# Where the weighted LoRA rows are split into high and low parts: before the transposes or behind them

## What is computed

```
xn  = layernorm(x)
K,V = elu(xn wk.T + bk) + 1, xn wv.T + bv;  KV = sum over the tokens of K V      (16 heads of 32)
out = Q KV / (Q sum K + 1e-8), then wo.T + bo;  Q = elu(xn wq.T + bq) + 1
s   = sigmoid(xn W_router) (8 experts); the best 2 of s + expert_bias get weights s / (sum of the two + 1e-8)
gate/up = xn W + (xn sA) sB / 8 + sum over experts of weight * (xn A_e) B_e / 8   (rank 8, width 1376)
ffn = (silu(gate) * up) W_down + the same LoRA terms of the down side
y   = x + attention + ffn
```

## Time and profile before

| What | Value |
|---|---|
| median of 3 runs | 721.21 us (720.41 to 721.88) |
| the profiled execution | 720.7 us, its span 718.9 us |
| TensorE busy | 701.2 us (98%) |
| VectorE busy | 376.2 us (52%) |
| ScalarE busy | 260.7 us (36%) |
| GpSimd busy | 122.3 us (17%) |
| granted clock of TensorE | 1.0 in the whole span |

### The profile page before, as it was taken

How to read it: one execution, slowest core, us unless ns; L and a number is a source line. 1 busy time by engine, 2 the same in 40 slices (tenths; PEclk the granted TensorE clock), 3 DMA queues, 4 the chain that set the end, 5 groups by cost and what they waited for, 6 DMA issues and landing times.

```text
span 718.9 us, 10792 instructions
## 1 busy us (share of the span) xinstructions
PE 701.2 (98%) x3690; PEld 563.2 (78%) x3690; DVE 376.2 (52%) x715; ACT 260.7 (36%) x402; POOL 122.3 (17%) x293
## 2 busy tenths in 40 slices
PE   7999999989999999999999999999999999999997
PEld 5788888876776677888888888888888888888886
DVE  5666556677575675444427444336534435544434
ACT  4344334564331432333333333324333224323322
POOL 3554555420642651000000000000000000000000
PEclk9999999999999999999999999999999999999999
DMA  7756656326746635000010500001600001300001
GB/s 241 270 194 195 202 192 210 125 111 251 274 142 236 221 131 217 18 0 0 0 49 37 208 0 0 0 4 54 233 0 0 0 0 58 117 0 0 0 0 60
DMA packets 22755, 72.79 MB, mean 101 GB/s; under 512 B 2688, under 2 KB 2944, under 8 KB 20688
## 3 DMA queue, kind: packets, MB, share of 16 engines
q1 hardware_dynamic: 22560, 72.24, 28.4%
q0 software_dynamic: 176, 0.30, 0.2%
HBM read 51.56 MB, written 20.97 MB: 101 GB/s over the span
## 4 chain that ended last, share of the span: by engine, by line
PE 90%; DVE 4%; issue 2%; POOL 2%; ACT 1%; DMA 1%; SPq 0%; DVEq 0%; POOLq 0%; ACTq 0%
PE bank L1115 19%; PE bank L1116 19%; PE bank L1117 19%; PE bank L1328 17%; PE bank L1303 6%; PE bank L1315 4%; PE bank L1228 2%; DMA w_raw<-in_wkT 1%; PE bank L1180 1%; PE bank L1132 1%; PE bank L1152 1%; PE bank L1144 1%; PE bank L1236 1%; PE bank L1344 0%; PE bank L1346 0%
## 5 line engine op out<-in xcount | busy, mean ns | idle before, releaser
L1115 PE MATMUL bank<-x,up_h 128*128 (+1 forms) x352 | 137.5, 391 | 2.1 <-DVE qf L980 1.2
L1116 PE MATMUL bank<-x,up_h 128*128 (+1 forms) x352 | 137.3, 390 | 0.0
L1117 PE MATMUL bank<-x,up_l 128*128 (+1 forms) x352 | 137.0, 389 | 0.0
L1048 DVE TENSOR_TENSOR hf<-bank,silu 128x512 f32<-128x512 f32 x44 | 30.4, 692 | 162.3 <-issue 142.6
L1115 PEld LDWEIGHTS bank<-x,up_h 128*128 128x128 f32 x352 | 66.1, 188 | 18.8 <-issue 2.1
L597 ACT ACTIVATE hid_h<-hf 128x512 fp32r<-128x512 f32 x44 | 27.8, 632 | 142.9 <-DVE hf L1048 142.9
L1117 PEld LDWEIGHTS bank<-x,up_l 128*128 128x128 f32 x352 | 66.1, 188 | 14.1
L1116 PEld LDWEIGHTS bank<-x,up_h 128*128 128x128 f32 x352 | 66.1, 188 | 13.8
L793 DVE TENSOR_TENSOR up_l<-up_raw,up_h 128x1024 fp32r<-128x1024 f32 x45 | 55.6, 1235 | 31.4 <-ACT up_h L597 31.4
L1328 PE MATMUL bank<-dn_h,hid_h 128*128 128x512 f32 x176 | 69.5, 395 | 0.0
L1328 PE MATMUL bank<-dn_l,hid_h 128*128 128x512 f32 x176 | 69.1, 392 | 0.0
(11 more groups left out here) (167 smaller groups left out, 1228.3 us busy)
## 6 DMA issues: line engine op xcount, KB each, us to landing
x<-scr_x SPq DMA_DIRECT2D x8, 2048.0 KB, 7.5
up_raw<-in_ffn_up SPq DMA_DIRECT2D x11, 768.0 KB, 5.5
scr_x<-xt SPq DMA_DIRECT2D x16, 512.0 KB, 4.4
xin<-in_x SPq DMA_DIRECT2D x16, 256.0 KB, 5.8
scr_z<-zt SPq DMA_DIRECT2D x16, 256.0 KB, 2.2
x3r<-in_x SPq DMA_DIRECT2D x16, 256.0 KB, 3.5
scr_att<-x3r SPq DMA_DIRECT2D x16, 256.0 KB, 2.1
z<-scr_z SPq DMA_DIRECT2D x4, 1024.0 KB, 5.0
```

What stands on the lines that cost most here:

```text
L1048: nc.vector.tensor_tensor(hf[:], ps_u[:], silu[:], ALU.mult).then_inc(h_done, 1)
L1115: nc.tensor.matmul(dst, lh, rh, start=start, stop=False, **kw)
L1116: nc.tensor.matmul(dst, lh, rl, start=False, stop=False, **kw)
L1117: return nc.tensor.matmul(dst, ll, rh, start=False, stop=stop, **kw)
```

## The change

The weighted rows are written unrounded into `zst`, now one block of 128 columns a side, the shared ones three times in the same operation. Two transposes a tile, one a side, take the place of four. The split is made behind them: ScalarE rounds the transposed rows from PSUM to `zt` in two operations (all 128 rows as the second block, the upper 64 as the first block's high half), and VectorE's `lora_lo` writes the low parts to partitions 64 to 127: a subtraction for the first block, and for the second one operation that multiplies the rounded rows by a mask (-1 for the 8 low rows, 0 elsewhere) and adds the transposed ones. The store now waits for VectorE. `lora_hi` is gone, `lora_lo` works on tile t-2 in the stage of tile t, and behind the stage it has new places. The low shared rows move by 8, and the prepared weights with them.

```diff
@@ -58,7 +58,7 @@
-SL = ER + R
+SL = ER + 2 * R
...
-        zf = at("zf", [P, 2, ER])
-        zs = at("zs", [P, 2, R])
-        zst = at("zst", [P, 2, 2, P], F32R)
+        zst = at("zst", [P, 2, P])
+        zmask = at("zmask_sb", [P, 1])
         zt = at("zt", [P, 2 * 2, P], F32R)
+        zt4 = zt[:].rearrange("p (a b) n -> p a b n", b=2)
...
-            nc.gpsimd.memset(zst[:].bitcast(F32), 0.0)
+            nc.gpsimd.memset(zst[:], 0.0)
...
             pool.dma_start(bq_c[:], dram["bq"]).then_inc(consts_in, 16)
+            pool.dma_start(zmask[:], dram["zmask"]).then_inc(consts_in, 16)
...
-            def lora_hi(t):
-
-                act.wait_ge(zf_done, t + 1)
-                round_to(zst[:, :, :, 0:ER], zf[:].unsqueeze(2).to_broadcast([P, 2, 2, ER]))
-                round_to(shared_cols(zst), zs[:].unsqueeze(2).to_broadcast([P, 2, 2, R])).then_inc(zhi_done, 1)
-
             def lora_out(t):
                 act.wait_ge(zt_ready, t + 1)
                 act.wait_ge(scr_zd, 16 * (t + 1))
-                round_to(zt[:].rearrange("p k n -> p (k n)"), ps_zt[:]).then_inc(zt_done, 1)
+                pst = ps_zt[:, 0:2 * P].rearrange("p (a n) -> p a n", a=2)
+                round_to(zt4[:, :, 1], pst)
+                round_to(zt4[0:ER, :, 0], pst[0:ER]).then_inc(zhi_done, 1)
...
-                if behind(t, 1):
-                    lora_hi(t - 1)
...
-            def stack_lo(st, zf_, zs_):
-
-                sub(st[:, :, 0, ER:2 * ER], zf_[:], st[:, :, 0, 0:ER])
-                return sub(st[:, :, 1, SL:SL + R], zs_[:], st[:, :, 1, SH:SH + R])
-
...
                 dve.wait_ge(route_done, t + 1)
-                nc.vector.tensor_scalar(zs[:], zraw[:, 2 * ER:2 * ER + 2 * R].rearrange("p (a r) -> p a r", a=2),
-                                        RSCALE, None, ALU.mult)
+                wait(dve, zt_ready, t)
+                shared = zraw[:, 2 * ER:2 * ER + 2 * R].rearrange("p (a o r) -> p a o r", a=2, o=1)
+                nc.vector.tensor_scalar(zst[:, :, SH:].rearrange("p a (b c) -> p a b c", c=2 * R)[:, :, 0:3, 0:R],
+                                        shared.to_broadcast([P, 2, 3, R]), RSCALE, None, ALU.mult)
...
-                        zf[:, a:a + 1].rearrange("p a (e r) -> p a e r", e=E),
+                        zst[:, a:a + 1, 0:ER].rearrange("p a (e r) -> p a e r", e=E),
                         zraw[:, a * ER:(a + 1) * ER].rearrange("p (a e r) -> p a e r", a=1, e=E), weight, ALU.mult)
-                last.then_inc(zf_done, 1)
+                last.then_inc(zst_done, 1)
 
             def lora_lo(t):
-                dve.wait_ge(zf_done, t + 1)
+
                 dve.wait_ge(zhi_done, t + 1)
-                stack_lo(zst, zf, zs).then_inc(zst_done, 1)
+                pst = ps_zt[:, 0:2 * P].rearrange("p (a n) -> p a n", a=2)
+                sub(zt4[ER:, :, 0], pst[0:ER], zt4[0:ER, :, 0])
+                nc.vector.scalar_tensor_tensor(zt4[ER:, :, 1], zt4[ER:, :, 1].bitcast(F32), zmask[ER:], pst[ER:], ALU.mult, ALU.add
+                                               ).then_inc(zt_done, 1)
...
-                if not first:
-                    lora_lo(t - 1)
+                if behind(t, 2):
+                    lora_lo(t - 2)
                 dve.wait_ge(z_ready, t + 1)
+                wait(dve, zst_done, t)
                 nc.vector.tensor_copy(zraw[:], ps_z[:, 0:NZ]).then_inc(zraw_done, 1)
...
-            dve.wait_ge(consts_in, 64)
+            dve.wait_ge(consts_in, 80)
...
             queries(0, (0,))
+            lora_lo(TILES - 2)
             m_lo(0, (2, 3))
...
             lora_weighted(TILES - 1)
-            lora_lo(TILES - 1)
...
             dve.wait_ge(rr_clear, 1)
+            lora_lo(TILES - 1)
             m_lo(1, (0, 1))
...
                 pe.wait_ge(zst_done, t + 1)
-                for k in range(4):
-                    last = nc.tensor.transpose(ps_zt[:, k * P:(k + 1) * P], zst[:, k // 2, k % 2, :].bitcast(F32), ident[:])
+                wait(pe, zt_done, t)
+                for k in range(2):
+                    last = nc.tensor.transpose(ps_zt[:, k * P:(k + 1) * P], zst[:, k, :], ident[:])
                 last.then_inc(zt_ready, 1)
...
+    zmask = np.zeros((P, 1), f32)
+    zmask[SL:SL + R] = -1.0
```

More of the change, by code:

```diff
@@ L60 @@
     "ffn_up": (P, FC, UPC), "ffn_dn": (P, FC, DNC), "b_dn": (P, 2, D),
-    "ident": (P, P), "headmask": (P, HC), "headcol": (P, KD, HEADS), "headrow": (P, KD, P), "earlier": (1, E, E),
+    "ident": (P, P), "headmask": (P, HC), "headcol": (P, KD, HEADS), "headrow": (P, KD, P), "earlier": (1, E, E), "zmask": (P, 1),
 }
@@ L249, in program @@
         rexp_done = sem("rexp_done")
-        zf_done = sem("zf_done")
         zhi_done = sem("zhi_done")
@@ L597, in round_to @@
                 return nc.scalar.activation(dst, src, ACT.Copy)
-            def shared_cols(st):
-                return st[:, :, 1, SH:].rearrange("p a (b c) -> p a b c", c=32)[:, :, :, 0:R]
             def tokens_hi(t, s, uses):
@@ L715, in _ @@
             queries(0, (1,))
-            lora_hi(TILES - 1)
             queries(0, (2, 3))
@@ L1405, in experts_out, with blocks @@
         return b.reshape(ER, b.shape[2])
-    def blocks(b, shared):
+    def blocks(b, shared, low=SL):
         full = np.zeros((P, 2, b.shape[1]), f32)
         full[0:ER, 0] = full[ER:2 * ER, 0] = full[0:ER, 1] = b
-        full[SH:SH + R, 1] = full[SL:SL + R, 1] = full[SH2:SH2 + R, 1] = shared
+        full[SH:SH + R, 1] = full[low:low + R, 1] = full[SH2:SH2 + R, 1] = shared
         return full
@@ L1438 @@
         "ffn_up": ffn_up, "ffn_dn": chunked(padded(ffn_dn, wide, DNC)),
-        "b_dn": blocks(experts_out(given["B_down"]), given["sB_down"]),
+        "b_dn": blocks(experts_out(given["B_down"]), given["sB_down"], ER + R),
         "ident": np.eye(P, dtype=f32), "headmask": np.repeat(np.eye(HC, dtype=f32), DK, axis=0),
         "headcol": headcol, "headrow": headrow,
-        "earlier": np.tril(np.ones((E, E), f32), -1).reshape(1, E, E),
+        "zmask": zmask, "earlier": np.tril(np.ones((E, E), f32), -1).reshape(1, E, E),
     }
```

## The result

The changed kernel takes 728.18 us (median of 4 runs, 727.53 to 728.55); the kernel before took 721.55 us beside it (4 runs, 720.41 to 723.07). The ratio on record is 1.0078, 95% interval 1.0057 to 1.0100 (the two medians divided give 1.0092, which lies inside the interval): slower, and by more than the forecast of 725.2 us and than its range, which ended at 727.0. The profiled execution took 727.53 us, 6.8 more than that of the kernel before.

A forecast was written before the change was run, and what follows sets the result against it. TensorE was taken to bound the token stage at 8.47 us a tile, with VectorE's loop at 8.22 taking over at 8.70. Stage +3.75 and behind it +0.25 gave +4.0: 725.2 us median, range 722.2 to 727.0.

The forecast's parts named there:

- the pace of 8.70 us: Token stage: VectorE's loop from one `zraw` to the next grows by 0.48 to 8.70 us a tile.
- the first of the twelve steps: Token stage, `zraw` of tile 1 to tile 2: taken as 8.70 us like the other steps up to tile 13.
- the +0.25 us behind the stage: From the token stage to the denominators: added and removed VectorE work and store waits together cost 0.25 us.
- TensorE's saving is hidden: Token stage: two transposes fewer cut TensorE's step by 0.22 to 8.25 us, hidden if VectorE's loop takes over.
- The loop takes over, and the two operations get no overlap: VectorE, `zs` to `zraw`: low-half operations of 0.42 and 0.48 us run without overlap, 1.87 us instead of 1.39.
- The surcharge for a PSUM source: VectorE's two low-half operations: some 0.06 us more each for reading PSUM, 1.6 us over the stage; not added.
- No cost on ScalarE: Token stage: ScalarE's two copies of `zt` end by 52.8 us, before the low halves need them at 53.4.
- `lora_lo` of tile 14: Behind the stage on VectorE, ahead of the comparison: the added low-half operations and a lost overlap cost +1.0 us.
- the wait for the store of tile 13's rows: Behind the stage: ScalarE waits for this store before rounding M, costing VectorE 0 to 1 us, taken as 0.35.
- The longer loop: Rival: a PSUM surcharge of 0.06 us on both operations, or the token load 1 us later; 726.3 to 728, chance 0.10.
- No hold: Rival: VectorE's two low-half operations overlap as others do, loop 8.41 us a tile, total 721.3 us; chance 0.12.
- TensorE as the bound: Rival: VectorE's loop stays at or below 8.25 us, so fewer transposes save 3.5 us, total 717.7; chance 0.08.

The follow-up runs named there:

- e3: Changed kernel with four transposes a tile again, the two added ones repeating the first two into space nobody reads; 729.81 us, ratio 1.0101.
- e1: Changed kernel with the two low-half operations writing partitions 0 to 63 instead of 64 to 127, low halves left out of the result; 723.50 us, ratio 1.0002.
- e9: Changed kernel with four tiny memsets on VectorE ahead of the token stage, shifting its loop in the instruction stream; 728.61 us, ratio 1.0076.
- e5: Changed kernel with short filler matmuls on TensorE before the places where it idled; 727.95 us, ratio 1.0064.
- e11: Changed kernel without the masked second low-half operation, that low half left out of the result; 720.63 us, ratio 0.9966.
- e12: Changed kernel with the two low-half operations right behind the copy of `zraw` instead of ahead of it; 721.99 us, ratio 0.9982.
- e6: Changed kernel with the two low-half operations one tile later, in VectorE's wait for the rank between `compare` and `select`; 718.33 us, ratio 0.9931.
- e10: e6 with ScalarE's `lora_out` of tile 14 moved behind its two `m_h` of the first half; 717.37 us, ratio 0.9925.
- e2: Changed kernel with long filler matmuls on TensorE, about twice those of e5, before the places where it idled; 729.12 us, ratio 1.0086.
- e7: e6 with the short TensorE fillers of e5; 719.26 us, ratio 0.9947.
- e8: Kernel before the change with only the short TensorE fillers of e5 added; 722.26 us, ratio 0.9992.

## Why the prediction was wrong in size and right in direction

Three terms of the sum failed: the pace of 8.70 us (1.0 us over the stage), the first of the twelve steps (0.6 us), and the +0.25 us behind the stage, in which a fall of the clock stood at nothing (1.2 us).

**TensorE's saving is hidden: right.** e3 gives the two transposes back and the pace stays at 8.79.

**The loop takes over, and the two operations get no overlap: right.** `zs` to `zraw` 1.88 against 1.87, the subtraction 0.418 us (0.42), the masked one 0.487 (0.48). The pairs in the earlier trace rows did carry over. By the Trainium skill, "VectorE: DVE Perf Modes", section "Two Vector instructions with no wait between them", this was the rule to expect; e1 agrees, by 0.36 us a tile. The surcharge for a PSUM source that the same page gives was not to be seen: 0.42 us for the subtraction from PSUM, as for the row of that shape from SBUF.

**No cost on ScalarE: right.** The two copies take 0.63 us together, and the low halves never wait for them in the loop.

**The loop's pace, 8.70: 0.09 too low, 1.0 us over eleven tiles.** e9 gives 0.05 of it to the place of VectorE's loop in the stream, which no sum of durations has. The rest stays open.

**"Then twelve steps of 8.70", from 29.16 - 0.55: the first of them was 9.27, 0.57 more.** The gain of 0.55 in the stage of tile 1 was real (7.56 instead of 8.14 between the first two), but `kb` of tile 2 then started 0.47 us late. In the profiled execution TensorE's K was late, made at half clock after an idle time of 1.5 us. But e3, which has no fillers and only two hidden transposes more, had a clock of 1.00 from 20 to 40 us in its trace and a step of 9.15: 0.35 us stood there without a releaser, as in e1, e5, e11 and e12. So of the 0.57 the clock has 9.27 - 9.15 = 0.12, and the pace 0.09; 0.36 is left, most of it the pause, which in e9 moved as the loop did. `zraw` of tile 13 was therefore at 134.46 and not 133.0, and the Wo products 5.3 us later and not 3.75.

**Behind the stage, +0.25: it measured 1.48, the largest miss.** Three terms were summed, and two are there: `lora_lo` of tile 14 with its lost overlap 1.06 (+1.0), and `bdn` 0.37 behind `zst` of tile 15 instead of 1.57 behind `zs` (-1.2, forecast -1.1). The third, 0.35 for the wait for the store of tile 13's rows, is not in this execution at all: ScalarE did not wait. Missing was the slow clock at the Wo and query products, which put the first `qf` at 6.79 us behind the first Wo product instead of 5.23, +1.56: the prediction had it at nothing. The 0.35 was no empty fear, since e5, e6, e11 and e12 have that wait: e6's end with it is 21.7, e10's without it 20.6. The two overlap, as e5 shows, whose end with the wait and a full clock is only 0.8 below that of the changed kernel.

**The rivals.** The longer loop was the nearest, 726.3 to 728, but for reasons that were not in it: its PSUM surcharge does not exist here, and the token load was not late at the queries. Its chance of 0.10 and the range's end at 727.0 were too low: the sum had been made from one execution in which the clock never fell, and only 0.5 us was set aside for it. No hold was wrong (e1). TensorE as the bound was wrong for this order and right for e6's, where 0.9 us of VectorE lies in a wait.

Together 1.0 + 0.6 + 1.2 = 2.8 us of miss on a forecast of +4.0, for the 6.8 of the two profiled executions. Some 1.7 of it is the clock, and there the choice of execution counts: the three runs of the changed kernel with a mean granted clock of 0.995 average 728.0 us and the 31 of the kernel before with the same, on three chips, 723.7. That is 4.3 apart and near the forecast of 4.0, but partly by luck, since the pause and the missing 0.09 a tile are in no term of it.

## What to carry to other kernels

Where an engine's loop closes over several engines, the sum that counts is that of the loop, and new work is free only in one of its waits: the same 0.9 us cost 0.44 us a tile ahead of `zraw`, and nothing in the wait for the rank. Before work is moved behind a hand-over, list the loop's waits with their lengths and put it into the longest; then look at who in the in-order queues waits for its result, since e10's single move was worth 1.1 us of path. And make the sum against more than one execution: a profile in which the clock never fell is the good case.

## What the runs showed of the hardware that was not expected

- The granted clock is part of a run's time even where no engine was changed. In the 59 runs of the kernel before beside these experiments, 31 have a mean granted clock of 0.995 and average 723.7 us; the 7 at 1.000 average 720.7. The profiled execution of before, at 1.00 throughout, had the same idle time of 1.5 us before tile 2 that in the changed kernel's was followed by a clock of 0.58; so the idle time is not enough to say whether it falls. e1, e3 and e12 had the same 1.5 us there and a clock of 1.00 from 20 to 40 us.
- Filling that idle time kept the clock at 1.00 or close to it (e2, e5, e7, e8), and in no kernel did it shorten the time by a measurable amount.
- Where VectorE's loop stands in the stream changed the start of one instruction by 0.13 us in every second tile (e9), with the same order and the same waits, and in the loop's first tile moved a pause of some 0.3 us from `kb` to `gt`.
- The store of tile 13's rows, behind the load of tokens on the same queue, released ScalarE 3.4 to 4.6 us after its issue in e1, e2, e5, e11 and e12, and had landed within 3.1 us in the changed kernel, e3 and e9; what makes the difference stays open.
